# Softmax probabilities moved in two tiles by eight DMAs a head pair, and the order planned anew

## What is computed

```python
xn = layernorm(x)                                   # (8, 512, 128)
# branch 1: causal attention, 16 heads of 64, rotary embedding on q and k
q, k, v = split(xn @ W_qkv); q, k = rotary(q), rotary(k)
weights = softmax(where(causal, q @ k.T / 8, -1e9)) # (8, 16, 512, 512)
a = (weights @ v) @ W_out
# branch 2: full attention, 16 heads of 8, then a mixture of 8 experts, the best 2 taken
y = xn + layernorm(attention(xn; Wq, Wk, Wv, Wo) ...)
f = y + layernorm(sum of the top 2 experts of y) ...
out = x + a + f
```

## Time and profile before

| | us |
|---|---|
| median of 3 runs | 1407.32 |
| lowest, highest | 1400.66, 1414.51 |
| the profiled execution | 1420.66 |
| its span, first to last instruction | 1418.8 |
| PE busy in the span | 1110.0 |
| DVE busy | 1034.0 |
| POOL busy | 857.6 |
| ACT busy | 742.4 |

### The profile page before, as it was taken

One profiled execution on the slowest core, in us unless ns is written; L12 is line 12 of the kernel. 1 busy time (PEld: TensorE's weight loads), 2 busy tenths in 40 slices (PEclk: granted clock), 3 DMA queues, 4 the chain that ended last, 5 costly groups with the idle time before them and its releaser, 6 DMA issues.

```text
span 1418.8 us, 23791 instructions
## 1 busy us (share of the span) xinstructions
PE 1110.0 (78%) x8474; PEld 662.9 (47%) x8474; DVE 1034.0 (73%) x2404; ACT 742.4 (52%) x1665; POOL 857.6 (60%) x728
## 2 busy tenths in 40 slices
PE   4778789687886878887798777877889678897866
PEld 2334446344452444544464444544546335463534
DVE  6966679767786767965788657777768766787646
ACT  3656455564544645555455644547545464555731
POOL 3658766657665485576564756656676555744940
PEclk8799979899798978988889886998969888698978
DMA  5163632455224442434524363244542245425342
GB/s 158 41 135 86 147 88 60 108 127 119 64 73 110 116 121 60 96 87 116 123 64 108 83 147 77 68 104 112 124 108 71 72 96 119 112 64 123 81 93 66
DMA packets 77793, 139.27 MB, mean 98 GB/s; under 512 B 11494, under 2 KB 23016, under 8 KB 77676
## 3 DMA queue, kind: packets, MB, share of 16 engines
q1 hardware_dynamic: 74204, 134.80, 39.8%
q10 hardware_dynamic: 3472, 2.95, 0.7%
HBM read 5.60 MB, written 2.10 MB: 5 GB/s over the span
## 4 chain that ended last, share of the span: by engine, by line
PE 36%; DVE 20%; DMA 17%; SPq 12%; POOL 7%; issue 4%; ACT 3%; ACTq 1%; POOLq 0%; DVEq 0%
DMA pt<-pn 12%; PE work L1708 10%; SPq L1140 10%; DVE fnmax L1458 7%; PE work L1758 4%; PE work L1694 4%; DVE pn L1588 4%; DMA swapped<-raw 4%; PE work L1616 3%; PE work L1724 3%; PE work L1618 3%; PE work L1617 3%; PE work L1733 3%; DVE work L1540 2%; DVE branch L1543 2%
## 5 line engine op out<-in xcount | busy, mean ns | idle before, releaser
L1196 POOL TENSOR_TENSOR raw<-raw,cos_t 128x512 f32<-128x512 f32 x128 | 163.5, 1277 | 406.4 <-DMA swapped<-raw 390.5
L1293 ACT ACTIVATE fpt<-work 128x1024 f32<-128x1024 f32 x256 | 251.9, 1026 | 202.0 <-PE work L1748 192.7
L1458 DVE TENSOR_REDUCE fnmax<-work 128x2 f32<-128x1024 f32 x256 | 302.4, 1215 | 59.1 <-PE work L1733 58.0
L1338 ACT ACTIVATE pn<-work,nmax 128x512 f32<-128x512 f32 (+3 forms) x512 | 266.0, 537 | 140.5 <-DVE nmax L1580 139.8
L1708 PE MATMUL work<-pt,v 128*32 128x384 f32 (+2 forms) x2560 | 211.9, 493 | 118.0 <-DMA pt<-pn 113.1
L1580 DVE CUSTOM_DVE_ANT_0 work<-work,causal 128x512 f32<-128x512 f32 (+3 forms) x512 | 236.6, 515 | 81.2 <-PE work L1694 80.8
L1708 PEld LDWEIGHTS work<-pt,v 128*32 128x32 f32 x2560 | 100.2, 136 | 228.4 <-issue 154.7
L1588 DVE STREAM_TRANSPOSE pn<-pn 128x1024 f32<-128x1024 f32 (+1 forms) x192 | 198.6, 1048 | 3.3 <-ACT pn L1338 3.2
L1211 POOL TENSOR_TENSOR qk_l<-raw,qk_h 128x512 fp32r<-128x512 f32 x128 | 180.0, 1413 | 3.4
L1200 POOL TENSOR_TENSOR raw<-raw,swapped 128x512 f32<-128x512 f32 x128 | 164.3, 1284 | 10.0
L1197 POOL TENSOR_TENSOR swapped<-swapped,sin_t 128x512 f32<-128x512 f32 x128 | 164.6, 1286 | 0.0
(11 more groups left out here) (153 smaller groups left out, 1893.0 us busy)
## 6 DMA issues: line engine op xcount, KB each, us to landing
pt<-pn SPq DMA_DIRECT2D x256, 320.0 KB, 5.7
swapped<-raw SPq DMA_DIRECT2D x256, 128.0 KB, 2.3
fqs<-fqn SPq DMA_DIRECT2D x96, 128.0 KB, 2.7
x_in<-in_L_attn_x_dram SPq DMA_DIRECT2D x8, 256.0 KB, 4.7
out_dram<-x_in SPq DMA_DIRECT2D x7, 256.0 KB, 2.3
fpt<-in_L_attn_W_qkv_dram ACTq DMA_DIRECT2D x3, 512.0 KB, 6.2
pn<-in_L_ffn_We_dram ACTq DMA_DIRECT2D x1, 512.0 KB, 9.7
wout<-in_L_attn_W_out_dram ACTq DMA_DIRECT2D x1, 512.0 KB, 12.5
```

The lines of the kernel that those rows point to most:

```text
L1196: nc.gpsimd.tensor_tensor(raw[:, n % 3], raw[:, n % 3], cos_t[:], ALU.mult)
L1293: nc.scalar.activation(fpt[:, ((b * G + g) * T + i) % FP, 2 * r:2 * r + 2].rearrange("p h n -> p (h n)"), bank_of(("fst", b, g, i), 2 * r, 2),
L1338: ins = nc.scalar.activation(pn[:, c % 2, :, h, tiles].rearrange("p c i r -> p i c r"), bank_of(("sc", b, c, unit), h)[:, at:at + n].rearr ...
L1458: nc.vector.tensor_reduce(fnmax[:, j, 2 * r:2 * r + 2, 0:1], bank_of(("fsm", b, g, j), 2 * r, 2).rearrange("p (f n) -> p f n", f=2), AX.X, ...
```

## The change

`pn` and `pt` become two tensors each. The first holds the tiles of units 0 and 1 (query tiles 3, 2 and 0, eight tiles), the second those of unit 2 (query tile 1, two tiles). `shuf` moves the first with four DMAs (2048 bytes a run, 256 KB a DMA) and waits only for `tr` of unit 1. A new step `shu2` moves the second with four DMAs (512 bytes a run, 64 KB a DMA) and waits for `tr` of unit 2. Both wait for `pv` of the pair before. `pv` waits for both, and query tile 1 has its own matmuls: 28 for 20 a pair. The four DMAs are issued in the order 0, 2, 1, 3. `turns` and the raw mask land in other tensors. `PLACE` and `PSUM` are new for nearly all steps; in `ORDER["SP"]` there are 301 steps for 237.

```diff
-TILES_OF = {3: 0, 2: 4, 0: 7, 1: 8}
-UNIT_TILES = [slice(0, 4), slice(4, 8), slice(8, 10)]
-PT_N = T * (T + 1) // 2
+PT_N = [2 * T, T // 2]
+PT_OF = {3: (0, 0), 2: (0, T), 0: (0, 2 * T - 1), 1: (1, 0)}
+UNIT_AT = [(0, slice(0, T)), (0, slice(T, 2 * T)), (1, slice(0, T // 2))]
...
-        pn = sb("pn", [P, 2, QUADS, 2, PT_N, STRIP])
-        pt = sb("pt", [P, QUADS, 2, PT_N, STRIP])
+        pn = [sb(f"pn{n}", [P, 2, QUADS, 2, tiles, STRIP]) for n, tiles in enumerate(PT_N)]
+        pt = [sb(f"pt{n}", [P, QUADS, 2, tiles, STRIP]) for n, tiles in enumerate(PT_N)]
...
-                elif kind == "shuf":
-                    c = x_[2]
-                    wait(sp, after("tr", b, c, 2))
+                elif kind in ("shuf", "shu2"):
+                    c, part = x_[2], int(kind == "shu2")
+                    wait(sp, after("tr", b, c, 1 + part))
                     wait(sp, after("pv", *ring(1, b, c, NC)))
-                    for a in range(QUADS):
-                        sp.dma_start(pt[:, a].rearrange("p h n r -> p (h n r)"),
-                                     pn[a * STRIP:(a + 1) * STRIP, c % 2].rearrange("p c h n r -> p c (h n r)")).then_inc(shuf_done[c % 2], 16)
+                    for a in (0, 2, 1, 3):
+                        sp.dma_start(pt[part][:, a].rearrange("p h n r -> p (h n r)"),
+                                     pn[part][a * STRIP:(a + 1) * STRIP, c % 2].rearrange("p c h n r -> p c (h n r)"))                            .then_inc((shuf_done, shu2_done)[part][c % 2], 16)
...
                     if b == 0:
+                        wait(act, after("tt", 0))
...
                         wait(act, landed("shuf", *ring(2, b, c, NC)))
+                        wait(act, landed("shu2", *ring(2, b, c, NC)))
...
                     wait(pe, landed("shuf", b, c))
+                    wait(pe, landed("shu2", b, c))
...
-                    for i, js in ((0, (3, 2, 1)), (0, (0,)), (1, (3, 2, 1)), (2, (3, 2)), (3, (3,))):
-                        first, at = TILES_OF[js[0]] + i, (T - 1 - js[0]) * P
+                    for i, js in ((0, (3, 2)), (0, (0,)), (0, (1,)), (1, (3, 2)), (1, (1,)), (2, (3, 2)), (3, (3,))):
+                        part, first = PT_OF[js[0]]
+                        first, at = first + i, (T - 1 - js[0]) * P
```

What the new order is shows in the places of one batch (batch 3; a number counts only against those of the same engine). DVE's `tr`, three units for each of eight pairs, and SP's steps:

```diff
     "tr": [
...
-        [463, 470, 477, 482, 496, 497, 505, 506, 515, 532, 534, 535, 545, 551, 552, 555, 556, 559, 574, 577, 578, 589, 594,
-         598],
...
+        [463, 470, 477, 482, 496, 498, 505, 516, 520, 525, 534, 535, 545, 548, 551, 555, 556, 562, 574, 576, 579, 590, 597,
+         600],
...
     "swap": [
...
-        [87, 88, 90, 92, 95, 96, 98, 99, 101, 103, 105, 107, 109, 112, 113, 116],
...
+        [107, 111, 114, 115, 118, 120, 123, 124, 125, 129, 132, 134, 135, 139, 140, 145],
...
     "shuf": [
...
-        [97, 100, 104, 108, 114, 115, 119, 123],
...
+        [122, 126, 130, 137, 142, 148, 149, 154],
...
+    "shu2": [
...
+        [121, 127, 133, 138, 143, 144, 150, 155],
...
     "pv": [
...
-        [436, 447, 464, 483, 497, 508, 518, 537],
...
+        [437, 447, 464, 481, 492, 510, 518, 536],
```

More of the change, by code:

```diff
@@ L58 @@
         [0],
[L59 to L64, removed]
+        [77],
+        [199],
+        [329],
+        [463],
+        [584],
+        [713],
         [842],
@@ L85 @@
         [86],
-        [213],
-        [342],
+        [212],
+        [343],
         [472],
-        [601],
+        [600],
         [729],
-        [858],
+        [859],
     ],
     "fv": [
[L94 to L101, removed]
+        [12],
+        [122],
+        [247],
+        [373],
+        [507],
+        [638],
+        [770],
+        [896],
     ],
     "fsm": [
[8 rows of a table removed]
[8 rows of a table added]
     ],
     "fmT": [
-        [14, 30, 58, 83],
@@ L182 @@
[L182 to L188, removed]
+        [48, 71, 97, 113],
+        [176, 200, 223, 242],
+        [305, 328, 349, 382],
+        [431, 457, 482, 503],
+        [563, 588, 610, 631],
+        [691, 717, 738, 760],
+        [820, 846, 865, 889],
+        [949, 974, 992, 1013],
     ],
     "pv": [
[8 rows of a table removed]
[8 rows of a table added]
     ],
@@ L426 @@
         [0],
-        [12],
-        [98],
-        [264],
-        [391],
-        [542],
-        [704],
-        [847],
+        [11],
+        [101],
+        [262],
+        [408],
+        [537],
+        [699],
+        [846],
     ],
@@ L442 @@
         [2],
-        [40],
+        [70],
         [216],
-        [364],
-        [509],
-        [650],
-        [801],
-        [945],
+        [361],
+        [506],
+        [656],
+        [803],
+        [944],
     ],
@@ L458 @@
         [6],
-        [91],
-        [227],
+        [92],
+        [232],
         [375],
-        [526],
-        [669],
-        [812],
-        [959],
+        [528],
+        [666],
+        [819],
+        [964],
     ],
     "sml": [
-        [3],
+        [7],
     ],
@@ L578 @@
+        [342, 374, 398, 431],
+        [488, 519, 547, 566],
+        [634, 665, 689, 712],
+        [781, 812, 838, 862],
+        [926, 957, 981, 1003],
+        [1071, 1101, 1118, 1142],
     ],
     "div": [
[8 rows of a table removed]
[8 rows of a table added]
     ],
     "yadd": [
-        [116, 188],
-        [263, 332],
-        [408, 479],
+        [118, 186],
+        [261, 333],
+        [409, 478],
         [554, 624],
-        [702, 772],
-        [845, 916],
+        [700, 772],
+        [847, 918],
         [991, 1062],
-        [1134, 1176],
+        [1133, 1176],
@@ L610 @@
         [163],
-        [308],
-        [455],
+        [309],
+        [454],
         [601],
         [746],
-        [893],
-        [1040],
-        [1149],
+        [892],
+        [1038],
+        [1150],
     ],
@@ L639 @@
     "gsub": [
-        [182],
+        [180],
         [327],
         [473],
-        [619],
-        [764],
-        [911],
-        [1057],
+        [618],
+        [763],
+        [910],
+        [1056],
         [1165],
@@ L679 @@
     "nm2": [
-        [229],
-        [360],
-        [520],
-        [666],
-        [813],
-        [948],
-        [1094],
+        [235],
+        [365],
+        [510],
+        [682],
+        [798],
+        [975],
+        [1092],
         [1178],
@@ L755 @@
     "res": [
-        [68],
-        [119],
-        [180],
-        [234],
-        [288],
-        [342],
+        [69],
+        [120],
+        [177],
+        [237],
+        [282],
+        [336],
         [394],
@@ L764 @@
     "rs2": [
-        [76],
-        [127],
-        [186],
+        [77],
+        [129],
+        [185],
         [240],
-        [294],
+        [290],
         [346],
-        [402],
+        [400],
         [429],
@@ L774 @@
     "out": [
-        [85],
-        [132],
-        [191],
-        [248],
-        [299],
-        [352],
-        [414],
+        [86],
+        [138],
+        [189],
+        [251],
+        [294],
+        [361],
+        [403],
     ],
     "swap": [
[8 rows of a table removed]
[8 rows of a table added]
     ],
     "fdup": [
-        [1, 3, 6, 13],
-        [24, 26, 34, 42],
-        [53, 61, 64, 72],
-        [81, 91, 94, 102],
-        [110, 118, 124, 131],
-        [144, 151, 154, 162],
-        [170, 181, 184, 192],
-        [201, 207, 212, 220],
+        [0, 3, 7, 15],
+        [24, 30, 42, 51],
+        [62, 68, 80, 90],
+        [104, 110, 119, 128],
+        [141, 147, 156, 166],
+        [175, 188, 194, 205],
+        [212, 228, 233, 242],
+        [249, 259, 269, 279],
     ],
     "shuf": [
[8 rows of a table removed]
[8 rows of a table added]
+    ],
[9 rows of a table added]
     ],
     "store": [
-        [46],
-        [73],
-        [106],
-        [138],
-        [166],
-        [223],
-        [232],
-        [236],
+        [58],
+        [95],
+        [131],
+        [176],
+        [206],
+        [262],
+        [289],
+        [300],
     ],
     "load": [
-        [50],
-        [76],
-        [111],
-        [143],
-        [171],
+        [60],
+        [102],
+        [136],
+        [177],
+        [216],
     ],
@@ L875 @@
     "POOL": ("rs0", "rs1", "rs2", "rope", "hi", "lo", "x2", "res", "out"),
-    "SP": ("swap", "shuf", "fdup", "store", "load"),
+    "SP": ("swap", "shuf", "shu2", "fdup", "store", "load"),
 }
@@ L882 @@
         KEYS[kind] = [(half,) for half in range(2)]
-    elif kind in ("div", "fan", "inv", "pv", "rT", "rb", "shuf"):
+    elif kind in ("div", "fan", "inv", "pv", "rT", "rb", "shuf", "shu2"):
         KEYS[kind] = [(c,) for c in range(NC)]
@@ L1043, in build @@
         shuf_done = [sem(f"shuf{n}_done") for n in range(2)]
+        shu2_done = [sem(f"shu2{n}_done") for n in range(2)]
         x_loaded = [sem(f"x{n}_loaded") for n in range(XB)]
@@ L1074, in landed @@
         def landed(kind, *key):
-            sems, per, dmas = (fdup_done, G, 3) if kind == "fdup" else (shuf_done, NC, QUADS)
```

(4 more changed lines are left out.)

366 lines of the change are left out of this document (180 added, 186 removed), and 413 rows, old and new, of tables (PLACE, PSUM).

## The result

| | before | after |
|---|---|---|
| median, us | 1406.02 (4 runs) | 1473.07 (4 runs, 1469.35 to 1477.0) |
| ratio after / before | | 1.0471, 95% interval 1.0407 to 1.0536 |
| span of the profiled execution, us | 1418.8 | 1467.9 |
| mean granted clock of TensorE in it | 0.861 | 0.849 |

The change costs 4.7%. The time lies outside the predicted range (1320 to 1430) and on the other side of the time before.

A forecast was written before the change was run, and what follows sets the result against it. Waits were taken as the bound, chiefly the probabilities' way from `pn` to `pt`, 22% of the span. Terms 64 - 13 + 14 + 8 = 73 us, half passing (37), gave 1370 us; range 1320 to 1430.

The forecast's parts named there:

- No help: Rival, chance 0.17: `pt` has one buffer, so early transposition may only meet a busy buffer; about 1405 us.
- (a): Way from unit 2's transposition to `pv`: 4.2 us where 9.6 were; 16 stretches at 4.0 us, 64 us gained.
- (b): SP's queue: four small issues cost 2.6 us a pair, net 1.8; swaps behind them come later, 13 us lost.
- (c): TensorE's clock: half of 16 stretches lose the standstill before `pv`, which then runs faster; 14 us gained.
- (d): TensorE's 28 matmuls for 20 a pair over the same 1280 columns: taken as 0, bound 60 us in all.
- (e): `pt` DMAs issued in order 0, 2, 1, 3: better rate, 0.7 us in 12 stretches, 8 us gained.
- Half of the sum passes: Whole kernel: of the 73 us sum, half, 37 us, was taken to arrive, since other waits take its place.
- The rival SP queue: Rival, chance 0.15: the queue stalls by rows; at 1.95 us a small issue the delay passes whole, 1455 us.
- Fixed cost for each DMA: Rival, chance 0.05: four small DMAs land one after another, 2.3 us each, needing 9.2 of 9.6 us; 1413 us.

The follow-up runs named there:

- e1_old_order: The changed kernel's new tiles, eight DMAs and 28 matmuls in the old order of all engines; ratio to the kernel before 0.9512, 1342.62 us.
- experiment 5: Changed kernel and e1_old_order with two of four DMAs of each size: 0.9009 and 0.8774 of the kernel before; with empty DMAs added, 0.9386 and 0.9177.
- e19_new_half_idle: Changed kernel with only two of the four DMAs of each size and two empty 4-byte DMAs behind each two; ratio to the kernel before 0.9386.

## Why the prediction was wrong

**The step that failed** is a term that the sum doesn't have: the new order itself was put at nothing. The change was costed as if tiles and DMAs alone changed; the new order entered only through the pairs that it turns or interleaves, and in the rival *No help* with "the plan's order of TensorE is nearly the old one (15.7 steps between the last scores and `pv`, before 16.2)". That is true, and it was the wrong engine. In (a) I took the 3.2 steps of VectorE between the transpositions of units 1 and 2 (before: 2.4) as a longer lead for the first four; but the same steps put unit 2's transposition later, and `pv` can't start before the DMAs that follow it. It ends 12.7 us behind its scores and not 9.7, so the time from it to TensorE's arrival at `pv` fell from 8.2 to 5.9 us. VectorE's new order could have shown it: between `max` and `tr` of unit 2 stand 6.6 steps on average where 5.4 stood, in the traces 4.9 us of work where 2.7 were. What the runs showed in place of nothing is a loss of 10% by the order, more than all terms of the sum together.

(a) *The way.* The parts are right: issue 0.60, landing 2.2, four of them 4.1 us (4.2 forecast; 5.3 in `e1_old_order`, where they follow the large four directly). The whole is wrong: 8.8 us in the median, not 4 to 6. The small four start with the large four and often a swap still ahead of them; the later of the fours begins to leave 3.5 us after its inputs in the mean, in 15 pairs the large four land last, and only in 42 of 64 pairs does a large issue start before unit 2 is transposed (in 21 more than 2.4 us before). I had counted the swap between the fours in 25 pairs as a gain for the swap in (b) and not as a delay here.

(b) *SP's queue.* 2.6 us a pair for the small issues was right (2.7 measured), the net was not: the trace's durations of the issues of `pt` and of the swaps add up to 546 us before and 562 after, 0.3 us a pair and not 1.8. The large four gave back 1.7 us a pair (5.0 to 3.3) where 0.8 were forecast, and the swaps' issues got shorter too (226 to 178 us in all). The measured price of an issue: 256 empty ones took 206 us of SP and 53 to 57 us of time (0.9009 to 0.9386 in the new order, 0.8774 to 0.9177 in the old, of some 1416 us).

(c) *The clock.* The mechanism was right, the sign followed the waits: a mean `pv` took 3.31 us before, 3.51 after, 2.78 in `e1_old_order`.

(d) *More matmuls.* Nothing forecast, a ratio of 0.9993 measured.

(e) *Order 0, 2, 1, 3.* 8 us forecast with an upper bound of 42; alone it gives 3.5%, some 50 us. The term was priced by the rate of the bytes in flight. What it changes is the hold of the queue: the median issue of `pt` falls by half and their sum from 320 to 267 us, while the swaps' median stays at 597 ns (their sum goes from 226 to 209 us). The Trainium skill, SBUF — State Buffer, "Can I just issue two DMAs to hit both halves?", says no: a DMA at partition 0 and one at partition 64, run together, were only 6% faster than one. Here four transfers from 32 partitions each landed 14% sooner (5.7 to 4.9 us) when neighbours in the queue lay in different halves. That the halves are the reason isn't shown; the order is.

*Half of the sum passes.* Without the new order the gain was 4.9%, 69 us of 1416.5 (the median of the kernel before, run beside it), against a sum of 73 and a forecast of 37: nearly all of the sum. The agreement is partly luck, since (e) was too small and (a) too large: the way fell by 1.6 us and not by 4 to 5.

*The rival SP queue* (1455) came near the number but not by its mechanism: only 12 of the 256 small issues take over 1.4 us (the longest 2.13), and SP's load does no more harm in the new order than in the old (experiment 5). *Fixed cost for each DMA* is out too: four small ones land 4.1 us after the first is issued, where one takes 2.2. The Trainium skill's advice to coalesce (DMA: Bandwidth & Descriptors, Rules for kernel authors) pointed the wrong way here: 1.25 MB a pair in eight DMAs instead of four gave 5% (0.9484 with the order 0, 1, 2, 3 kept). In the old order the large four leave ahead of unit 2's transposition in 48 of 64 pairs, which one DMA over both tiles could not.

## What to carry to other kernels

Where a change comes with a planned order, price the order first. For each hand-over between engines, add up the durations of what the new order sets between producer and user, and set it against the way that the trace shows, not the one the change hopes for; here a producer that came 3 us later, with its user left where it was, went with a loss twice as large as what the change had won. Look at both ends: the steps ahead of the user were nearly unchanged. Change the DMAs with the old order first, measure the way that results, and plan with that. And before splitting transfers, try another order of the same ones.

## What was not expected of the hardware

- The same four 320 KB DMAs in the order 0, 2, 1, 3 in place of 0, 1, 2, 3: median issue 1269 to 646 ns, landing 5.7 to 4.9 us, the kernel 3.5% faster. With 256 and 64 KB DMAs the median issue of the 256 KB ones fell from 959 to 687 ns, but the kernel's time didn't change by anything that could be measured.
- A DMA of 4 bytes in each of 32 partitions holds SP 0.6 us in the median and 0.8 in the mean (206 us for 256), and lands after 2.2 us, as long as one of 64 KB:

```profile
pt<-pn SPq DMA_DIRECT2D x128, 64.0 KB, 2.2
...
warm<-consts SPq DMA_DIRECT2D x256, 0.1 KB, 2.2
```

The fence is the page of `e19_new_half_idle`, part 6.
